# Second stage of a four-stage kernel: three pairs of buffers for gathered rows, gathers issued three experts ahead

## The reference

```python
# _L0_ffn_ref, h: 2048 tokens x 512
xb = zeros((E, CAP + 1, Hd)).at[eid, pos].set(h_rep)      # rows of each expert, E = 32, CAP = 192
g = einsum('ech,eih->eci', xb, w_gate)
u = einsum('ech,eih->eci', xb, w_up)
inter = silu(g) * u
yb = einsum('eci,ehi->ech', inter, w_down)
y = yb[eid, pos] * w_slot[:, None]
routed = y.reshape(-1, K, Hd).sum(axis=1)
```

## Time and profile before

| | |
|---|---|
| median of 3 runs | 1192.48 us |
| lowest and highest | 1188.62 and 1199.31 us |
| profiled execution | 1201.21 us, its span 1199.4 us |
| TensorE busy in the span | 1063.8 us, 89% |
| VectorE, ScalarE, GpSimd busy | 480.3, 331.4, 384.2 us |
| mean granted clock of TensorE | 0.938 |
| moved by DMA | 148.52 MB |
| chain that ended last | PE 64%, DMA 15% |

### The profile page before, as it was taken

One profiled execution on the slowest core, in us unless ns is written; L12 is line 12 of the kernel. 1 busy time (PEld: TensorE's weight loads), 2 busy tenths in 40 slices (PEclk: granted clock), 3 DMA queues, 4 the chain that ended last, 5 costly groups with the idle time before them and its releaser, 6 DMA issues.

```text
span 1199.4 us, 13046 instructions
## 1 busy us (share of the span) xinstructions
PE 1063.8 (89%) x4351; PEld 707.0 (59%) x4351; DVE 480.3 (40%) x1148; ACT 331.4 (28%) x529; POOL 384.2 (32%) x340
## 2 busy tenths in 40 slices
PE   5777969579979999999599999899799999999995
PEld 4333424168769888886276766656355566556553
DVE  5767687224324444432684756451111111111110
ACT  3444441023323443332223423211012221222221
POOL 0003767625444555553002002220023233233322
PEclk9867979879989999999899999999899999999998
DMA  9110111379989989984503104219822332333330
GB/s 329 77 53 23 32 36 45 97 266 258 249 267 277 248 240 249 245 198 59 194 18 41 66 9 45 36 37 293 364 37 55 71 62 51 66 68 57 58 71 8
DMA packets 52801, 148.52 MB, mean 124 GB/s; under 512 B 12244, under 2 KB 12628, under 8 KB 47297
## 3 DMA queue, kind: packets, MB, share of 16 engines
q1 hardware_dynamic: 24752, 81.09, 21.4%
q0 software_dynamic: 24160, 44.03, 19.2%
q10 hardware_dynamic: 3824, 22.57, 5.5%
HBM read 109.76 MB, written 41.08 MB: 126 GB/s over the span
## 4 chain that ended last, share of the span: by engine, by line
PE 64%; DMA 15%; DVE 8%; issue 4%; POOL 4%; ACT 3%; SPq 0%; ACTq 0%; POOLq 0%; DVEq 0%
PE pb L586 16%; PE pb L602 8%; DMA acc_rows<-big 7%; PE pb L456 6%; PE pb L559 6%; PE pb L315 5%; PE pb L317 5%; PE pb L316 5%; DMA big<-hn_rows,big 4%; PE pb L322 4%; PE pb L378 3%; DVE big L908 2%; POOL list_rows L1300 2%; DVE big L916 2%; POOL acc_rows L1331 2%
## 5 line engine op out<-in xcount | busy, mean ns | idle before, releaser
L586 PE MATMUL pb<-big 128*128 x624 | 193.7, 464 | 5.5 <-issue 5.5
L456 PE MATMUL pb<-big 128*128 128x192 f32 x1024 | 174.9, 330 | 2.1 <-ACT bigr L746 1.3
L456 PEld LDWEIGHTS pb<-big 128*128 128x128 f32 x1024 | 170.9, 193 | 6.1 <-issue 2.8
L586 PEld LDWEIGHTS pb<-big 128*128 128x128 f32 x624 | 116.7, 192 | 65.0 <-issue 8.0
L1331 POOL DMA_INDIRECT acc_rows<-big x64 | 95.9, 1498 | 138.8 <-DMA acc_rows<-big 47.8
L1300 POOL DMA_INDIRECT list_rows<-big x96 | 93.9, 978 | 139.0 <-DVE big L920 110.4
L315 PE MATMUL pb<-bigr 128*128 128x512 f32 (+2 forms) x320 | 132.2, 413 | 4.4 <-DVE bigr L908 3.5
L1358 POOL DMA_INDIRECT out<-big x39 | 61.8, 1585 | 207.3 <-ACT big L888 207.3
L316 PE MATMUL pb<-bigr 128*128 128x512 f32 (+2 forms) x320 | 127.5, 399 | 0.0
L317 PE MATMUL pb<-bigr 128*128 128x512 f32 (+2 forms) x320 | 127.3, 398 | 0.0
L916 DVE SCALAR_TENSOR_TENSOR big<-pb,big 128x512 f32<-128x512 f32 (+1 forms) x80 | 58.8, 735 | 143.4 <-PE pb L559 41.4
(11 more groups left out here) (124 smaller groups left out, 1160.7 us busy)
## 6 DMA issues: line engine op xcount, KB each, us to landing
big<-in_we SPq DMA_DIRECT2D x32, 1024.0 KB, 7.9
rawr<-in_we SPq DMA_DIRECT2D x32, 512.0 KB, 4.3
big<-in_we ACTq DMA_DIRECT2D x1, 8704.0 KB, 37.0
hn_rows<-big SPq DMA_DIRECT2D x32, 256.0 KB, 2.0
big<-in_we ACTq DMA_DIRECT2D x1, 6528.0 KB, 34.1
big<-in_x SPq DMA_DIRECT2D x4, 1024.0 KB, 15.4
acc_rows<-big SPq DMA_DIRECT2D x16, 256.0 KB, 4.7
big<-acc_rows SPq DMA_DIRECT2D x16, 256.0 KB, 4.3
```

The source lines that it names most:

```text
L456: r = e.matmul(ps[:, m * CAP:(m + 1) * CAP], WR[b % 4][:, at_:at_ + 128], XT[b % 2][:, k, :], start=(k == 0), stop=(k == 3))
L586: r = e.matmul(ps[:, 0:I1], XT1[b % 2][:, k, :], W1[:, bass.ds(r0 + (q * 4 + k) * I1, I1)], start=(k == 0), stop=(k == 3))
```

## The change

Two more half buffers, G[4] and G[5], take the last free 1024 words of the stage's space, so that three pairs are used in turn. Expert n uses pair n mod 3 and waits for `turn.n-3`. GpSimd's list becomes `fetch.2`, then `fetch.n+3`, `add.n-1` for each n. The new buffers lie where the first stage kept the tokens that its last stores read, so `fetch.2` also waits until all stores into ACC have landed (eight semaphores). The gathers of the second stage have six semaphores, those of the fourth stage two of their own.

```diff
--- before.py
+++ after.py
@@ -204,12 +204,13 @@
 
 
         two = taker(0, T * D)
-        G = [None, None, two(D, p1=HALF), two(D, p1=HALF)]
+        G = [None, None, two(D, p1=HALF), two(D, p1=HALF), None, None]
         XT = [two(4, CAP) for _ in range(2)]
 
         INS, SSS = two(2, D), two(D)
         G[0], G[1] = two(D, p1=HALF), two(D, p1=HALF)
         YS = [two(D, p1=HALF) for _ in range(4)]
+        G[4], G[5] = two(D, p1=HALF), two(D, p1=HALF)
         LB = ring(HALF, 2, p1=64)
         MN = [S(MN0 + 512 * i, D) for i in range(4)]
         WDH, WDL = [R(13056, 1024), R(14080, 1024)], [R(15104, 1024), R(16128, 1024)]
@@ -272,7 +273,8 @@
         l_hn = [[sem(f"l_hn{b}{q}") for q in range(2)] for b in range(4)]
         l_acc = [[sem(f"l_acc{b}{q}") for q in range(2)] for b in range(4)]
         l_list0, l_lb, l_list1, l_lb1 = sem("l_list0"), sem("l_lists_back0"), sem("l_list1"), sem("l_lists_back1")
-        l_g = [sem(f"l_gather{i}") for i in range(4)]
+        l_g = [sem(f"l_gather{i}") for i in range(6)]
+        l_g4 = [sem(f"l_rows{i}") for i in range(2)]
         l_rd = [sem(f"l_down{i}") for i in range(3)]
         l_add = [sem("l_add0"), sem("l_add1")]
         l_sgu, l_w1 = sem("l_sgu"), sem("l_w1")
@@ -289,7 +291,7 @@
         dve2 = "split.0 " + words(lambda n: f"mulu.{n} " + (f"slo.{n - 14} " if 14 <= n < 22 else "")
                                 + (f"turn.{n + 1} " if n + 1 < E0 else "") + f"spi.{n} " + (f"yout.{n - 1} " if n else "")
                                 + (f"split.{n + 1} " if n + 1 < E0 else ""), E0) + f"yout.{E0 - 1}"
-        pool2 = words(lambda n: (f"fetch.{n + 2} " if n + 2 < E0 else "") + (f"add.{n - 1}" if n else ""), E0) + f" add.{E0 - 1}"
+        pool2 = "fetch.2 " + words(lambda n: (f"fetch.{n + 3} " if n + 3 < E0 else "") + (f"add.{n - 1}" if n else ""), E0) + f" add.{E0 - 1}"
         sp2 = "dw.0 dw.1 fw.2 dw.2 fw.3 " + words(lambda n: (f"dw.{n + 3} " if n + 3 < E0 else "") + (f"fw.{n + 4}" if n + 4 < E0 else ""), E0)
         pe4 = "turnt.0 " + words(lambda n: f"upt.{n} " + (f"turnt.{n + 1} " if n + 1 < NT else "") + (f"downt.{n - 1} " if n else "") + f"flipt.{n}", NT) + f" downt.{NT - 1}"
         act4 = "turnt.0 " + words(lambda n: f"silut.{n} " + (f"turnt.{n + 1} " if n + 1 < NT else "") + (f"yt.{n - 1}" if n else ""), NT) + f" yt.{NT - 1}"
@@ -428,8 +430,8 @@
                 elif kind == "turn":
                     g = GF if b == 0 else G
                     for h in range(2):
-                        s = (2 * b + h) % 4
-                        e.wait_ge(l_g[s], 16 * (b // 2 + 1))
+                        s = (2 * b + h) % 6
+                        e.wait_ge(l_g[s], 16 * (b // 3 + 1))
                         if b == 0:
                             e.wait_ge(s_dve, dv("ids0"))
                             e.wait_ge(s_dve, dv("accx", 1, 3))
@@ -566,7 +568,7 @@
                     e.transpose(Q[0][:, 64:64 + NT], LB1v[:, :, 1], ident[0:NT, 0:NT]).then_inc(s_pe, c.up())
 
                 elif kind == "turnt":
-                    e.wait_ge(l_g[b % 2], 16 * (E0 // 2 + b // 2 + 1))
+                    e.wait_ge(l_g4[b % 2], 16 * (b // 2 + 1))
                     if b == 0:
                         e.wait_ge(s_dve, dve_end3)
                     else:
@@ -1310,10 +1312,11 @@
                         e.wait_ge(s_dve, dv("accx", 1, 3))
                     elif b == 2:
                         e.wait_ge(s_dve, dve_end1)
-                    if b >= 2:
-                        e.wait_ge(s_pe, pe("turn", b - 2))
+                        stores_landed(e, l_acc)
+                    if b >= 3:
+                        e.wait_ge(s_pe, pe("turn", b - 3))
                     for h in range(2):
-                        s = (2 * b + h) % 4
+                        s = (2 * b + h) % 6
                         off = bass.IndirectOffsetOnAxis(ap=IDI[0:HALF, 2 * b + h:2 * b + h + 1], axis=0)
                         e.indirect_dma_start((G if b else GF)[s], None, HN, off).then_inc(l_g[s], 16)
                 elif kind == "add":
@@ -1347,7 +1350,7 @@
                         e.wait_ge(l_h2[1], 128)
                     if b >= 2:
                         e.wait_ge(s_pe, pe("turnt", b - 2))
-                    e.indirect_dma_start(G1[b % 2], None, HN2, bass.IndirectOffsetOnAxis(ap=IDI[:, b:b + 1], axis=0)).then_inc(l_g[b % 2], 16)
+                    e.indirect_dma_start(G1[b % 2], None, HN2, bass.IndirectOffsetOnAxis(ap=IDI[:, b:b + 1], axis=0)).then_inc(l_g4[b % 2], 16)
                 elif kind == "addt":
                     e.wait_ge(s_act, av("yt", b))
                     if b == 0:
```

## The result

| | before | after |
|---|---|---|
| median | 1191.99 us (1188.62 to 1199.31, 4 runs) | 1218.08 us (1212.94 to 1222.82, 4 runs) |
| profiled execution, its span | 1201.21, 1199.4 us | 1222.82, 1221.0 us |
| last landing of the second stage | 569.57 us | 589.54 us |
| mean granted clock of TensorE | 0.938 | 0.939 |

The ratio is 1.0219, 95% interval 1.0157 to 1.0281. The forecast was 1188.5, between 1172 and 1200: the sign was wrong. Ratios leave out runs over 1.5% above the fastest of their kernel: one in experiment 2, seven in 10, and five of the 36 runs of before beside experiments 5 to 11.

The account below looks back on a forecast made before the run. The second stage was taken as paced by GpSimd's ring of adds; three losses, 1.0 + 1.8 + 1.2 = 4.0 us, would return and all else count nothing. That gave 1197.2 us profiled, 1188.5 median, range 1172 to 1200.

Parts of the forecast that it names:

- The ring of adds: Second stage, GpSimd: each expert's adds wait for the previous pair's landing; rounds of 1.77 + 7.0 + 0.73 = 9.5 us.
- Where the stall goes: Second stage: gather path lifted one round, TensorE up to 10 us ahead, then held by yout; ScalarE's and VectorE's waits grow.
- SP's loads keep their place: GpSimd's new order: no queue is passed by anything else, so SP's weight loads were taken as unmoved.
- The rounds themselves stay if the traffic beside them does: Second stage's add rounds: weights one expert sooner against the adds, same bytes, taken at nothing; bounds 2.7 us either way.
- TensorE's waits for rows: Second stage: TensorE's 22.4 us of waits for gathered rows fall to little more than the head's 4.0 us.
- The three losses of 4.0 us: Second stage: adds delayed by their expert's output, 1.0 us at 353.56 and 1.8 + 1.2 us at the end, all return.
- The head and the new wait: Stage start: extra gathers cost 2.5 us and fetch 2's store checks 0 to 1.5 us, both hidden in 9.12 us idle.
- C: Rival for the second stage: nothing moves, as heavier rounds take the gain at the end; 1192 us, chance 0.15.
- A: Rival: all TensorE's lost time returns, beat 8.64 us, stage gives back 18.4 to 28.6 us; 1164 to 1174, chance 0.12.
- B: Rival: TensorE's lap, held by yout and a lower clock, exceeds the adds' round; 1205 to about 1211 us, chance 0.07.

Follow-up runs that it names:

- experiment 2: Changed kernel with load fw ahead of load dw in SP's list: 1198.96 us against 1213.77 for the kernel before, ratio 0.9848.
- experiment 10: Changed kernel with fw ahead of dw in SP's list, twelve runs on another chip: median 1200.89 us, faster group 0.9884 of the kernel before.
- experiments 5 to 11: Follow-up runs of the changed kernel, its variants and variants of the kernel before, on one chip where before took 1195.2 to 1195.9 us.
- experiment 1: Changed kernel with split.n+1 ahead of yout.n-1 on ScalarE and VectorE: 1201.03 us against 1213.77 for the kernel before, ratio 0.9872.
- experiment 8: Changed kernel with half of the up block's products left out, all loads kept: one run, 1221.3 us.
- (9): Changed kernel with four down-weight buffers instead of three: six runs, 1178.99, four between 1197.21 and 1203.58, one of 1585.63 us; no ratio given.
- (11): Kernel before with VectorE's yout waiting for the second add one expert later than it must: 1224.92 us against 1195.9, ratio 1.0248.
- 12: Changed kernel with fw ahead of dw in SP's list, a third time, for a profile: 1190.44 us beside 1211.55 for before, one run each.

## Why the prediction was wrong

**The bound: right.** The ring of adds paces the stage, and it still does: 1.77, the landing of the second add, 0.73. What was wrong was to treat the landing of 7 us as given. It goes with when the loads are issued: over the sixteen rounds the second add lands in 8.6 us in the changed kernel, in 7.1 before, in 6.9 in experiment 1 and in 6.0 in 10 (medians).

**Where the stall goes: right, and not followed to its end.** "ScalarE's and VectorE's waits for acc_rows, 1.6 us now, grow to many": they grew to 128.5 + 31.5 = 160.0 us where "some 10 us or more" was named. (The 1.6 us was ScalarE's alone; with VectorE's 4.6 it was 6.2 us, so the wait that now does the harm was there before, small and unread.) The gather path was lifted as said: TensorE's `up` of expert 11 starts at 346.72 in place of 360.51, 13.8 us earlier, in the rows

```profile
346.72 2.60 PE L458 MATMUL pb<-big 128*128 128x192 f32 x15
```

```profile
360.51 3.74 PE L456 MATMUL pb<-big 128*128 128x192 f32 x22
```

after and before. That lead didn't last: the last `up` starts at 561.37, 13.9 us behind the 547.52 of before, where the prediction put it some 10 us ahead. For the argument then asked what TensorE does behind `yout`, and not what VectorE's and SP's queues hold there. "SP's loads keep their place" is true of the list and false of the time.

**The step that failed** is "The rounds themselves stay if the traffic beside them does", with "The bytes are the same, and I take this at nothing", between bounds of 2.7 us either way. The bytes were the same; their moment was not. The 2.7 priced one round that is loaded or not, once. What the runs showed in its place: `yout`, held to a landing, held `split`, `dw` and `fw` to it too, so the loads fell on the second add, which landed in 8.6 us in place of 7.1, in every one of sixteen rounds: 16 x 1.48 = 23.7 us. A bound for a thing that recurs must be taken per round and then multiplied.

**TensorE's waits for rows** were to fall from 22.4 us to 4; they are 30.5. TensorE ran a round ahead, and there the gather behind the previous add is just in time again. It is harmless: in experiment 8 these waits grew to 84.9 us and the time did not.

**The three losses of 4.0 us: right where they can be seen.** The 1.8 + 1.2 us at the end returned, and a little more: 3.65 us over the last six rounds. The chain there is the landing and the issue of the next pair, with no output in it:

```profile
576.85 4.09 DMA acc_rows<-big
580.94 2.58 issue
583.53 1.40 POOL acc_rows L1334
```

Landing and issue make 4.09 + 2.58 = 6.67 us, near the 6.8 that the prediction worked out. There are no loads left here, and so no lock.

**The head and the new wait: right.** `fetch.2` (249.76) starts 1.59 us behind the gather before it, put down to VectorE and not to the stores; before, it stood there 1.50 us for VectorE too. `fetch.3` (252.19) follows in the queue's usual 0.30 us, and the first add comes 0.44 us later, after an idle time of 9.13 us.

**The rivals.** C, no change, is out. A didn't happen, but its condition, landings of 6.1 us or below, was real: with the loads off the landing the second add lands in 6.3 us in experiment 2 and in 6.0 in 10 (medians), and TensorE's beat of 8.64 is reached or nearly so. The prediction had taken the landings as fixed. The Trainium skill's "Perfetto Trace Analysis", section Optimization Strategy, would make the dependency behind the bound engine's gaps start sooner; that was done here, the gathers came a round earlier, and the time rose by 26.1 us. B had the right place, what stands "queued behind" a held `yout`, and a time not far off (1205 to 1211), but the wrong price: not TensorE's clock, whose mean over the stage was 0.96 of the full 2.4 GHz before (243 to 570 us) and after (243 to 590 us) alike, but SP's loads behind `split`.

**What the loop needs** was shown by taking its links away one at a time: `split` behind `yout` (1), `fw` behind `dw` (2), `dw` behind the last `split` (9), and by making it in the kernel before (11). Each round time is that of one profiled execution; the kernels without the lock lie at 8.7 to 9.9, those with it at 11.0 to 11.2. That the second add lands 4 us slower than the first because it shares the DMA engines with the loads is read from the windows; it was not measured by itself. How the lock first forms, near expert 8, wasn't tried.

## What to carry to other kernels

When a wait is lifted, list what is queued behind the next wait on that engine, and behind everything which that releases on the other queues, DMA loads above all: a prefetch can tie loads to a landing that they were free of. Ask of a ring of DMAs when the traffic beside it starts, not only how much it is. If one queue holds two loads with different causes, try the one whose cause comes first ahead: that gave the shortest rounds here (experiments 2, 10 and 12), though not in every execution the shortest time.

## What was not expected of the hardware

- An add of 96 rows took 4.4 us to land (4.1 to 4.6 over the sixteen rounds) when issued into nearly idle DMA engines, and 8.3 us (7.8 to 9.6) when 1.5 MB of loads were issued within 0.4 us of it. With the same bytes bunched, the DMA share was 0.70 (mean of 0.68, 0.76, 0.59 and 0.77 in four windows of 10 us after) in place of about 0.92 (0.94, 0.87, 0.89 and 0.96 before).
- The kernel before takes 1195 to 1196 us on one chip and 1212 to 1214 on two others, with mean granted clocks of 0.932 to 0.943 on the first and 0.931 to 0.937 on one of the latter. A gain of 1% is seen only against runs on the same chip.
- With the loads freed (experiment 10), one kernel has executions of 1181 to 1184 and of 1199 to 1205 us on one chip at clocks of 0.935 to 0.943; the cause is open.
